# A graph stage with its PSUM banks dealt out anew, its TensorE order changed, and one addition moved from GpSimd to VectorE

## The reference

```python
x = x + gnn(layernorm(x), adj, ...)          # x: (32, 256, 128)
x = x + ffn(layernorm(x), ...)

def gnn(x, adjacency):
    agg = epsilon * x + einsum('bnm,bmd->bnd', adjacency, x)
    h = einsum('bnd,dh->bnh', agg, W1) + b1            # H = 512
    h = silu(h * rsqrt(mean(square(h)) + eps) * rms_weight)
    return einsum('bnh,hd->bnd', h, W2) + b2

def ffn(x):                                            # 8 experts, top 2
    logits = flat @ router_w.T
    gates, idx = top_k(softmax(logits), 2)             # normalised over the two
    h = silu(x @ w1[e].T) * (x @ w3[e].T)
    return sum over the two experts of gate * (h @ w2[e].T)
```

## Time and profile before

| | us |
|---|---|
| median of 3 runs | 606.42 (605.57 to 607.59) |
| span of the profiled execution | 646.6 |
| steps 2 to 7 of the graph stage, 36.86 to 81.96 | 45.10 |
| steps 8 to 27, the loop, 81.96 to 267.49 | 185.53 |
| expert stage, from about 325 to 592 | 267.00 |
| last stage, 592 to 646.6 | 54.60 |

### The profile page before, as it was taken

The page is one execution under the profiler, slowest core; times in us unless marked ns, Lnnn a source line. Parts: engine busy times, 40 slices in busy tenths (PEclk is TensorE's granted clock), DMA queues, the critical chain, the costliest instruction groups (busy, mean ns, idle before and its releaser), DMA issues.

```text
span 646.6 us, 13636 instructions
## 1 busy us (share of the span) xinstructions
PE 544.2 (84%) x3859; PEld 475.5 (74%) x3860; DVE 391.2 (60%) x1394; ACT 320.7 (50%) x701; POOL 384.1 (59%) x440
## 2 busy tenths in 40 slices
PE   6899989988999899995389999999999999897000
PEld 5567766666676666774389999999999999897000
DVE  3466664665566556665646666666666666464465
ACT  3366654455455555654145545545455455352343
POOL 5337765666576667667516777776777676577000
PEclk8699996899888989997679999999999999899555
DMA  5223321423232132311312222222222222121798
GB/s 140 64 73 108 120 85 50 125 73 102 72 109 85 57 122 74 108 35 42 117 56 69 69 76 70 77 69 65 82 66 78 69 65 72 59 68 44 218 312 254
DMA packets 66942, 59.76 MB, mean 92 GB/s; under 512 B 8407, under 2 KB 60890, under 8 KB 66918
## 3 DMA queue, kind: packets, MB, share of 16 engines
q1 hardware_dynamic: 57558, 41.10, 22.3%
q0 software_dynamic: 8640, 17.84, 8.3%
q10 hardware_dynamic: 720, 0.53, 0.3%
HBM read 35.42 MB, written 24.02 MB: 92 GB/s over the span
## 4 chain that ended last, share of the span: by engine, by line
PE 72%; DMA 6%; issue 5%; POOL 5%; ACT 4%; DVE 3%; another core or an unknown queue 2%; SPq 1%; DVEq 0%; POOLq 0%; ACTq 0%
PE route_ps L798 13%; PE up_ps L692 11%; PE up_ps L782 8%; PE up_ps L784 8%; PE up_ps L783 7%; PE up_ps L657 5%; PE up_ps L678 4%; DMA ew_sb<-results 3%; PE up_ps L677 3%; PE up_ps L680 3%; PE rowt_ps L769 2%; PE route_ps L709 2%; POOL expert_rows L458 2%; PE up_ps L679 2%
## 5 line engine op out<-in xcount | busy, mean ns | idle before, releaser
L507 POOL DMA_INDIRECT results<-result,dest x142 | 138.6, 976 | 34.9 <-issue 28.2
L458 POOL DMA_INDIRECT expert_rows<-rows,slot x128 | 125.9, 983 | 37.0 <-issue 34.2
L782 PE MATMUL up_ps<-rows_lo,up_hi 128*114 128x256 f32 x426 | 127.1, 298 | 3.8 <-DVE rows_lo L1032 3.8
L783 PE MATMUL up_ps<-rows_hi,up_lo 128*114 128x256 f32 x426 | 121.2, 285 | 0.0
L784 PE MATMUL up_ps<-rows_hi,up_hi 128*114 128x256 f32 x426 | 120.9, 284 | 0.0
L615 ACT ACTIVATE scaled<-up_ps 114x768 f32<-114x768 f32 x71 | 57.7, 813 | 116.6 <-PE up_ps L784 114.2
L798 PE MATMUL route_ps<-ew_sb,hidden_t 114*128 x852 | 106.8, 275 | 0.7 <-DVE result L1047 0.7
L798 PEld LDWEIGHTS route_ps<-ew_sb,hidden_t 114*128 114x128 f32 x852 | 100.7, 192 | 0.9 <-issue 0.9
L445 POOL TENSOR_TENSOR inverse<-spreads,minus_half 128x6 f32<-128x6 f32 (+2 forms) x37 | 46.0, 1243 | 70.3 <-DVE spreads L826 63.5
L1032 DVE TENSOR_TENSOR rows_lo<-rowt_ps,rows_hi 128x256 fp32r<-128x256 f32 x71 | 30.2, 425 | 92.5 <-ACT rows_hi L620 89.8
L692 PE MATMUL up_ps<-w_sb,hidden_t 128*128 128x128 f32 x512 | 82.1, 309 | 0.0
(11 more groups left out here) (121 smaller groups left out, 888.5 us busy)
## 6 DMA issues: line engine op xcount, KB each, us to landing
slot_rows<-expert_rows SPq DMA_DIRECT2D x71, 130.0 KB
adj<-in_adj_t SPq DMA_DIRECT2D x32, 256.0 KB
ew_sb<-results SPq DMA_DIRECT2D x32, 256.0 KB, 4.0
tokens<-in_x SPq DMA_DIRECT2D x32, 128.0 KB
out<-tokens SPq DMA_DIRECT2D x16, 256.0 KB, 3.6
ew_sb<-in_ew SPq DMA_DIRECT2D x6, 456.0 KB
results<-result,dest POOLq DMA_INDIRECT x142
expert_rows<-rows,slot POOLq DMA_INDIRECT x128
```

Of the source, the lines that this page charges most:

```text
L458: pool.indirect_dma_start(out=expert_rows, out_offset=bass.IndirectOffsetOnAxis(ap=slot[:, r, n:n + 1], axis=0), in_=rows[:, r, n // TT, n ...
L507: pool.indirect_dma_start(out=results, out_offset=bass.IndirectOffsetOnAxis(ap=dest[:, r, h:h + 1], axis=0), in_=result[:, r, h, :], in_of ...
L782: pe.matmul(part, up_hi[:, r, at], rows_lo[:, r, :], start=True, stop=False)
L783: pe.matmul(part, up_lo[:, r, at], rows_hi[:, r, :], start=False, stop=False)
```

## The change

- `up_ps` now holds four tiles of `hid_ps` (two for even graphs, two for odd ones), one bank `hidt_ps` for both transposes of a graph, and `agg_ps`. `y_ps` has a bank of its own, and `rowt_ps`, `route_ps` and `rank_ps` share one, `routing_ps`.
- `first_product` waits for the scaling of the graph two before. `transpose_hidden` is cut in two calls; each waits for the Silu that read the shared bank last. The order of PE becomes rows, hidden 0, router, rank, hidden 1.
- `add_epsilon` moves from POOL to DVE, behind `agg_low`, which itself moves ahead of `shift` and `scale_hidden`.
- On POOL the power comes behind the waits for slots.
- `bias_cut` has 128 partitions, zero but for the first three, cleared by a memset of POOL at the start; the bias matmuls run over 128 rows.
- In the expert stage `result_ps` and `slots_ps` are in other banks, still two different ones.

```diff
-        bias_cut = sb("bias_cut", [3, BIAS], BF16)
+        bias_cut = sb("bias_cut", [P, BIAS], BF16)
...
-        agg_ps = up_ps[0][:, 0:512]
-        hid_ps = [up_ps[0][:, (1 + t) * 512:(2 + t) * 512] for t in range(TT)]
-        hidt_ps = [up_ps[1][:, t * 512:(t + 1) * 512] for t in range(TT)]
-        y_ps = up_ps[1][:, 2 * 512:3 * 512]
-        rank_ps = y_ps[:, TT * D:TT * D + TT * E]
-        rowt_ps = bank("rowt_ps", [P, 512])
-        route_ps = bank("route_ps", [P, 512])
+        hid_ps = [[up_ps[(2 * r + t) // 3][:, (2 * r + t) % 3 * 512:((2 * r + t) % 3 + 1) * 512] for t in range(TT)]
+                  for r in range(2)]
+        hidt_ps = up_ps[1][:, 512:2 * 512]
+        agg_ps = up_ps[1][:, 2 * 512:3 * 512]
+        y_ps = bank("y_ps", [P, 512])
+        routing_ps = bank("routing_ps", [P, 512])
...
             def step(j):
-                if has_inverse(j):
-                    inverse_of(j)
                 sent = j.plus(-4)
                 if sent.within(GRAPHS):
                     pool.wait_ge(s_slot, sent.plus(1).n)
                     pool.wait_ge(s_row1, sent.plus(1).n)
                     pool.wait_ge(s_rowdest, sent.plus(1).n)
-                if j.plus(3).within(GRAPHS):
-                    add_epsilon(j.plus(3))
+                if has_inverse(j):
+                    inverse_of(j)
                 if sent.within(GRAPHS):
                     send(sent)
...
+            def transpose_hidden(u, t):
+                pe.wait_ge(s_scaled, u.n * TT + t + 1)
+                if t > 0 or positive(u.n):
+                    pe.wait_ge(s_silu, u.n * TT + t)
+                for c in range(HC):
+                    ins = pe.transpose(hidt_ps[:, c * P:(c + 1) * P],
+                                       scaled[:, u.ring(2), t, c * P:(c + 1) * P], ident[:, :])
+                ins.then_inc(s_hidt, 1)
...
-                    if positive(u.n):
-                        pe.wait_ge(s_scaled, u.n * TT + t - 1)
+                    if positive(u.plus(-1).n):
+                        pe.wait_ge(s_scaled, u.plus(-2).n * TT + t + 1)
-                    pe.matmul(hid_ps[t][:, :], ones[0:3, :], bias_cut[:, 0:H], start=True, stop=False)
+                    pe.matmul(hid_ps[r][t], ones[:, :], bias_cut[:, 0:H], start=True, stop=False)
...
                 if j.within(GRAPHS):
-                    transpose_hidden(j)
-                if j.plus(-3).within(GRAPHS):
-                    rank(j.plus(-3))
-                if j.plus(-2).within(GRAPHS):
-                    router(j.plus(-2))
+                    transpose_hidden(j, 0)
+                if j.plus(-2).within(GRAPHS):
+                    router(j.plus(-2))
+                if j.plus(-3).within(GRAPHS):
+                    rank(j.plus(-3))
+                if j.within(GRAPHS):
+                    transpose_hidden(j, 1)
...
+                if j.plus(2).within(GRAPHS):
+                    agg_low(j.plus(2))
+                if j.plus(3).within(GRAPHS):
+                    if isinstance(j.k, int) and j.off == -3:
+                        dve.wait_ge(s_epsid, 1)
+                    add_epsilon(j.plus(3))
                 if has_inverse(j):
```

More of the change, by code:

```diff
@@ L416, in _ @@
             pool.memset(minus_half[:, :], -0.5).then_inc(s_const, 1)
+            pool.memset(bias_cut[:, :], 0.0).then_inc(s_biaszero, 1)
             pool.wait_ge(s_mem, 2)
@@ L658, in sum_neighbours @@
                 ins.then_inc(s_agg, 1)
-            def transpose_hidden(u):
-                for t in range(TT):
-                    pe.wait_ge(s_scaled, u.n * TT + t + 1)
-                    for c in range(HC):
-                        ins = pe.transpose(hidt_ps[t][:, c * P:(c + 1) * P],
-                                           scaled[:, u.ring(2), t, c * P:(c + 1) * P], ident[:, :])
-                    ins.then_inc(s_hidt, 1)
+            def transpose_hidden(u, t):
[6 more added lines that the diff above has]
+                ins.then_inc(s_hidt, 1)
             def first_product(u):
@@ L686, in second_product @@
                     pe.wait_ge(s_x2, u.n)
-                if positive(u.plus(-2).n):
-                    pe.wait_ge(s_place, u.plus(-2).n)
                 for t in range(TT):
-                    pe.matmul(y_ps[:, t * D:(t + 1) * D], ones[0:3, :], bias_cut[:, H:H + D], start=True, stop=False)
+                    pe.matmul(y_ps[:, t * D:(t + 1) * D], ones[:, :], bias_cut[:, H:H + D], start=True, stop=False)
                     for c in range(HC):
@@ L698, in transpose_rows @@
                 pe.wait_ge(s_row0, u.plus(1).n)
+                if positive(u.n):
+                    pe.wait_ge(s_logitc, u.n)
+                if positive(u.plus(-1).n):
+                    pe.wait_ge(s_place, u.plus(-1).n)
                 for t in range(TT):
@@ L753, in _ @@
             run_steps(pe, 1, G["steady"], G["bodies"], G["last"], step)
-            pe.matmul(rowt_ps[:, 0:E], ones[:, :], taken[:, TILES, :], start=True, stop=True).then_inc(s_cnt, 1)
+            pe.matmul(y_ps[:, 0:E], ones[:, :], taken[:, TILES, :], start=True, stop=True).then_inc(s_cnt, 1)
             pe.wait_ge(s_ew2, 16 * (GRAPHS // UNROLL - 2))
@@ L821, in agg_low, with add_epsilon @@
                                   ALU.subtract).then_inc(s_agglo, 1)
+            def add_epsilon(u):
+                dve.wait_ge(s_adjin[u.ring(2)], u.turn(2) * 16 + 16)
+                blocks = adj[:, u.ring(2), :, :].rearrange("p c (b n) -> p (c b) n", n=P)[:, 0:TT * TT:TT + 1, :]
+                dve.tensor_tensor(blocks, blocks, eps_ident[:, :].unsqueeze(1).to_broadcast([P, TT, P]),
+                                  ALU.add).then_inc(s_adj, 1)
             def mean_square(u):
@@ L832, in scale_hidden @@
                 for t in range(TT):
-                    dve.scalar_tensor_tensor(out=scaled[:, r, t, :], in0=hid_ps[t][:, :], scalar=inverse[:, r, 2 * TT + t:2 * TT + t + 1],
+                    dve.scalar_tensor_tensor(out=scaled[:, r, t, :], in0=hid_ps[r][t], scalar=inverse[:, r, 2 * TT + t:2 * TT + t + 1],
                                              in1=rms_w_sb[:, :], op0=ALU.mult, op1=ALU.mult).then_inc(s_scaled, 1)
@@ L896, in step @@
                     dve.wait_ge(s_x[fresh.ring(4)], fresh.turn(4) * 16 + 16)
-                if j.plus(2).within(GRAPHS):
-                    agg_low(j.plus(2))
-                if is_fresh:
                     for t in range(TT):
@@ L972, in _ @@
             dve.wait_ge(s_cnt, 1)
[L973 removed]
+            dve.tensor_copy(counts[:, :], y_ps[:, 0:E]).then_inc(s_tab, 1)
             dve.wait_ge(s_tab, 1)
```

38 lines of the change are left out of this document (16 added, 22 removed).

## The result

The changed kernel takes 589.57 us (584.59 to 592.23, 4 runs) where the kernel before takes 607.0 (605.57 to 608.57, 4 runs): a ratio of 0.9713, 95% interval 0.9675 to 0.9751. The forecast was 620.4 us, slower; it was wrong in sign. In later groups of runs the kernel before itself took 646 us (one group) and 664 to 665 us (two groups), and in these last two the changed kernel took 672 (ratios 1.0089, 1.0051 to 1.0128, and 1.0108, 1.0036 to 1.0179). So there are two conditions, and they have to be held apart: in the *on-time* one before takes 607 us, in the *late* one more. Experiment 4 is about them. Until then all numbers are from the on-time condition, unless it says otherwise.

A forecast was written before the change was run, and what follows sets the result against it. TensorE bounds written-out steps; profiled loop steps are bound by a circle through POOL with a late release. On-time sum: 30 x 0.56 = 16.8, -3, -1, +1, rounded to 14 on 606.4: 620.4 us, range 596 to 631.

The forecast's parts named there:

- Bias over 128 partitions: In the bias matmuls, weight loads go from 91 to 97 ns, worth nothing; clock effect -1 us, bounds -5 and 0.
- TensorE's order: On TensorE, half the filling is left before the router, which idles 0.55 us for normed_t: +0.56 us a step.
- T: End of the second first product on TensorE, 64.45 us in the written-out step; times in a step count from it.
- Four banks: On TensorE at start-up, the first product no longer waits for `scaled`: -3 us, bounds -5 and 0; nothing later.
- Eps on DVE: The add leaves POOL (0.73 us) for DVE (about 0.42); shift moves back 1.4 us, covered by 0.9: nothing.
- Power behind the slots: On POOL, the power waits for slots; loop circle 9.83 us against 9.06, +0.77 a loop step if late release stays.
- the late case: Loop where TensorE's release reaches ACT 0.86 us after POOL's last DMA issue, as profiled; sum +18.0 us.
- Drain: At the end of the graph stage, the power of step 32 waits for slots: +1 us, bounds 0 and 2.
- the 40 us: Profiled span, 646.6 us, is 40.2 above the 606.42 median; unprofiled runs estimated short of most of the loop's 34.7 excess.
- Rival A: Loop's late release was in timed runs and vanishes; steps 8.10 us, 585 us, 596 with half; chance 0.15.
- Rival B: Clock and start-up at good bounds (-10), 0.2 us of router's wait hidden: about +1, 606 to 609 us; chance 0.12.
- Rival C: TensorE's new idle spots lower the clock once per ten steps more; 633 us with late release; chance 0.10.

The follow-up runs named there:

- Experiment 4: Reruns of the kernel before, the changed kernel and variants, some written out, to study the two conditions; late: before 664.37 us, changed 672.25.
- b_eps: Kernel before with the eps add on DVE ahead of shift and the power behind the slot waits: 607.48 us, ratio 1.002.
- a_bias3: Changed kernel with the bias matmuls over 3 rows again: 620.8 us, ratio 1.0221.
- b_eps_bias128: Kernel before with the 128-row bias, the eps add on DVE and the power behind the slot waits: 623.55 us, ratio 0.9667, beside a before of 645.63.
- b_bias128: Kernel before with only the bias over 128 rows: 584.23 us, ratio 0.963.
- b_best_flat: Kernel before with 128-row bias, eps add on DVE behind the scaling, power first, a one-column POOL addition, graph stage written out: 575.92 us, ratio 0.949.
- after_3: Changed kernel run again without edits, in the late condition: 671.66 us, ratio 1.0108 beside a before of 664.95.
- before_2: Kernel before run again without edits for a second profile, in the late condition: 664.37 us.
- b_best: Kernel before with 128-row bias, eps add on DVE behind the scaling, power first, a one-column POOL addition: 631.76 us, ratio 0.977, beside a before of 645.63.

## Why the prediction was wrong, step by step

- **Bias over 128 partitions: the step that failed.** It said that the loads "go from 91 to 97 ns ... the loads run beside matmuls, so nothing", and took -1 us with bounds of -5 and 0. It measured 620.8 - 589.57 = 31.2 us, and the steps compared, 8.05 against 6.98 us, both ran at clock 1.00. The error was to price a load by its duration and not by what it does to its neighbours. The sign stood in the trace of before: the 512-column bias L677 is followed after 0.31 us, while L679, over as many columns, is followed after 0.22. I took the spans between TensorE's starts as they stood and never asked why they were uneven, because TensorE counted as busy in them.
- **TensorE's order, +0.56 a step: right.** From b_eps (7.53) to a_bias3 (8.05 in a written-out step) it is 0.52. The banks are in this difference too. The idle time at the router was sized 0.55 and is 0.40, because the four transposes ahead of it end at T + 0.66 and not at T + 0.50; the router itself starts at T + 1.05, as worked out. In a_bias3 the last first product starts at 61.37 and takes 0.40, and the next sum starts at 63.86: 2.09 us after it, where 2.08 was worked out.
- **Four banks, -3 at the start: within its bounds with 3-row loads, nothing with full ones.** In b_eps a first product waits 2.09 us for `scaled`, and the fourth sum starts at 28.36 us; in a_bias3 that product starts at 19.11 without a wait and the sum at 23.92, 4.4 earlier. But b_eps_bias128, with two banks, has the sum at 22.39, and the changed kernel at 25.20. From 12 to 20 us the clock is 0.50 in b_eps, 0.59 in a_bias3, 0.67 in the changed kernel and 1.00 in b_eps_bias128. So the clock at the start weighs as much here as the wait; what sets it was not taken apart.
- **Eps on DVE, covered: right** (b_eps, ratio 1.002). That this edit becomes worth something once TensorE is faster, 7.08 us a step in b_bias128 against 6.5 in b_best_flat, the prediction did not ask: it priced each part against the bound of before.
- **Power behind the slots, +0.77 in the late case: not shown.** Loop steps of 9.83 were forecast there, against 9.06; after_3 has 9.75 and before_2 9.40 on the mean, 0.35 more, with the banks and TensorE's order in it. The pair that differs in the orders of POOL and DVE points the other way: 8.28 us with the power behind the slots (b_eps_bias128), 8.74 with it first (b_best). The 18 us that the sum gave for the late case came out as 7 to 8.
- **Drain, +1: right in size, by luck.** From the last sum to the copy of the counts it takes 34.2 us in b_eps and 35.7 in a_bias3. But the power stands behind the slots in both, and in before, where it does not, it takes 34.1. So the order of POOL is not the reason.
- **Reading the 40 us.** The prediction worked out both conditions and took the lower sum, that of the on-time one, on an estimate. The runs bear the estimate out. Without the bias term its sum is 621, against 620.8 in a_bias3; that it comes so near is in part luck, for the order is some 1 us under its term, the start 1.4 better than its term in the profiles, and the drain 0.5 worse.
- **Rival A** came near in time (585) for a reason that was not there: the timed runs had no late release that could vanish. **Rival B** gave the bias only a gain of the clock, and its time was too high. **Rival C**, a falling clock, fell: 1.00 through the whole loop, with a gap of 0.40 us in each step. The rule of the Trainium skill that stood beside it ("TensorE: Matmul & The Clock Gate", A second HAM failure mode: psum-queue depth-cycling) has no case in the loop of the on-time profile.

Of the signs that the prediction named, the wait at the router is there, for it; the loop step under 9 us, the square that follows its product at once in the loop (100.97 us, after a product that ends at 100.94) and the clock line without dips in the first half are there too, against it.

## What to carry to other kernels

A matmul over fewer than 128 rows (3 and 64 were run) between full ones is not cheap: count the changes between partial and full rows, and either fill the rows with zeros (here 128 matmuls, 31 us) or put the partial ones together. A timeline that shows an engine as busy does not show that it is at its pace: compare start-to-start times of neighbours of the same size, and ask for the cause of each uneven one before pricing an edit there. Price each part of a change also against the next bound, and judge a profile by its span before its loop is taken for that of the timed runs.

## What was not expected of the hardware

- Matmuls over 3 rows among full ones cost TensorE 0.23 to 0.27 us for each group (busy 7.04 us a step with two groups, 7.65 with four, 6.58 with none), and three in a row cost no more than one; over 64 rows a step is as long as over 3.
- TensorE's semaphore updates can come up to 2.5 us late (after_3) while POOL issues indirect DMAs, and half of the late ones come 0.9 to 1.1 us after the end of one. The same program shows none of it in other runs, and the same chip has been seen in both conditions.
- In the condition with a before of 664 us the expert stage slows down too: TensorE was busy in 180.82 of 190 us between 330 and 520 us (before_2), where b_eps has it busy in all 190. In the group with a before of 646 us it was not slower: b_best there has all 190.
- POOL's add over two SBUF inputs holds up DVE beside it: in b_bias128 `shift` starts at 120.59, 0.05 us into the add, and takes 0.69, until the add ends; in the changed kernel it takes 0.16. `chosen`, which takes 0.73 there (from 119.90), stands beside the end of POOL's power and not beside the add; in the changed kernel it runs in the middle of the power and takes 0.19. Why only some of them are held up was not taken apart.
